# Moving the weight casts of a fused attention and expert kernel from its projection stage to the head of its attention stage, and doubling the final output buffer

## The reference, cut to what matters

```python
def _L0_attn_ref(x, Wq, bq, Wk, bk, Wv, bv, Wo, bo):      # 16 heads of 128, causal
    q = (x @ Wq.T + bq).reshape(B, S, nh, hd).transpose(0, 2, 1, 3)
    ...
    probs = jax.nn.softmax(scores, axis=-1)
    attn = jnp.einsum('bhqk,bhkd->bhqd', probs, v)
    y = attn.transpose(0, 2, 1, 3).reshape(B, S, H)
    return y @ Wo.T + bo

def _L0_ffn_ref(x, router_w, ...):                        # 8 experts, top 2
    ...
    combined = jnp.einsum('etf,te->tf', expert_out, full_w.reshape(-1, E)).reshape(B, S, D)
    out = jnp.einsum('bsd,df->bsf', combined, proj_w) + proj_b
    y = x + out
    rms = jnp.sqrt(jnp.mean(y * y, axis=-1, keepdims=True) + EPS)
    return norm_w * (y / rms)

xn = _layernorm(x, axis=-1)
x = x + _L0_attn_ref(xn, ...) + _L0_ffn_ref(xn, ...)
```

## Time and profile before

| | us |
|---|---|
| two timed executions | 5594.8 and 5755.85 |
| their median | 5675.32 |
| the profiled execution, its own time | 5243.77 |
| span of its slowest core, from first to last instruction | 5242.2 |
| spans of its 8 cores | 5219.3 to 5242.2 |

### The profile page before, as it was taken

How to read it: one execution, slowest core, us unless ns; L and a number is a source line. 1 busy time by engine, 2 the same in 40 slices (tenths; PEclk the granted TensorE clock), 3 DMA queues, 4 the chain that set the end, 5 groups by cost and what they waited for, 6 DMA issues and landing times.

```text
span 5242.2 us, 52589 instructions; the slowest of 8 cores (5219.3 to 5242.2 us)
## 1 busy us (share of the span) xinstructions
PE 4232.7 (81%) x18602; PEld 1734.9 (33%) x18602; DVE 1166.2 (22%) x1883; ACT 1007.8 (19%) x1781; POOL 336.3 (6%) x539
## 2 busy tenths in 40 slices
PE   0169999999634899999994448888988889897988
PEld 0134444444321344444442213333333332323333
DVE  2431111211121111211122122212131221314211
ACT  2511111111111111111112111230403214040400
POOL 1001111111011111111111100000000000000000
PEclk9999999999867899999997778998989989897899
DMA  8214444444866544444466830000000000001033
GB/s 126 81 29 65 69 69 69 69 69 68 134 125 131 90 69 68 69 69 69 69 97 135 149 104 17 17 9 25 5 21 13 13 21 5 25 9 60 26 121 121
DMA packets 223346, 339.65 MB, mean 65 GB/s; under 512 B 16578, under 2 KB 189042, under 8 KB 217714
## 3 DMA queue, kind: packets, MB, share of 16 engines
q0 software_dynamic: 156368, 201.47, 26.7%
q1 hardware_dynamic: 66722, 134.82, 8.0%
HBM read 487.34 MB, written 75.50 MB: 107 GB/s over the span
## 4 chain that ended last, share of the span: by engine, by line
PE 72%; DMA 12%; DVE 5%; DVEq 4%; ACT 3%; issue 2%; another core or an unknown queue 1%; ACTq 1%; SPq 0%; POOL 0%; POOLq 0%
PE pbk L243 72%; DMA wring<-pwb 7%; DVEq L129 4%; DMA xcst<-x 2%; DMA prt<-out 2%; ACT xnstg L375 1%; DVE wTst L693 1%; DVE WoT L759 1%; ACT rrow L813 1%; ACTq L129 1%; DVE pstg L616 1%; DMA xst<-x 1%; ACT rrow L816 0%; DVE finst L866 0%
## 5 line engine op out<-in xcount | busy, mean ns | idle before, releaser
L243 PE MATMUL pbk<-wring,xnT 128*128 128x512 bf16 x8192 | 1861.1, 380 | 65.8 <-DMA wring<-ew 64.0
L243 PEld LDWEIGHTS pbk<-wring,xnT 128*128 128x128 bf16 x8192 | 760.4, 98 | 1031.1 <-issue 187.3
L243 PE MATMUL pbk<-xnT,wTst 128*128 128x512 bf16 x3072 | 753.5, 411 | 0.0
L491 DVE SCALAR_TENSOR_TENSOR comb<-silu,fullw,comb 128x512 f32<-128x512 bf16 x448 | 336.7, 751 | 1400.6 <-ACT silu L479 1400.3
L791 ACT ACTIVATE PTs<-pbk 128x512 bf16<-128x512 f32 x640 | 382.3, 597 | 1335.5 <-PE pbk L243 1306.3
L479 ACT ACTIVATE silu<-pbk 128x512 bf16<-128x512 f32 x512 | 305.6, 597 | 1634.1 <-PE pbk L243 1600.5
L243 PEld LDWEIGHTS pbk<-xnT,wTst 128*128 128x128 bf16 x3072 | 320.2, 105 | 413.1 <-issue 109.7
L243 PE MATMUL pbk<-wring,cT 128*128 128x512 bf16 x1024 | 249.8, 407 | 185.0 <-DMA wring<-pwb 184.0
L248 POOL DMA_DIRECT2D wring<-ew x256 | 192.0, 750 | 2039.0 <-PE pbk L243 2039.0
L243 PE MATMUL pbk<-sIb,wring 128*128 128x128 bf16 x1024 | 118.0, 258 | 223.8 <-DVE wTst L693 125.4
L243 PE MATMUL pbk<-PTs,Vh 128*128 128x512 bf16 x640 | 257.6, 403 | 0.0
(11 more groups left out here) (100 smaller groups left out, 1869.3 us busy)
## 6 DMA issues: line engine op xcount, KB each, us to landing
wring<-ew POOLq DMA_DIRECT2D x256, 512.0 KB, 6.0
wring<-pwb SPq DMA_DIRECT2D x64, 512.0 KB, 8.3
wring<-wqk SPq DMA_DIRECT2D x64, 512.0 KB, 3.2
xcst<-x POOLq DMA_DIRECT2D x64, 256.0 KB, 4.4
out<-pstg SPq DMA_DIRECT2D x64, 256.0 KB, 3.0
prt<-out SPq DMA_DIRECT2D x16, 1024.0 KB, 6.8
out<-finst SPq DMA_DIRECT2D x16, 1024.0 KB, 4.7
xst<-x SPq DMA_DIRECT2D x32, 256.0 KB, 4.1
```

The costliest lines, as they stand in the source:

```text
L243: return eng.matmul(b, l, r, start=st, stop=sp)
L491: return e.scalar_tensor_tensor(co, silu_sb[ssl][:], wcol, co, ALU.mult, ALU.add)
```

## The change

**Where the casts are issued.** In the projection stage each of the 16 column blocks had four casts ahead of it, 64 in all. Now a list `EARLY` holds 12 of them (the rows of Wq, Wk and Wv for heads 0 to 3), and each of the first 12 blocks has one. The last four blocks have none. The other 52 stand in the attention stage, at the head of the loop over pairs of heads: those of two later heads for Wq, Wk and Wv, and two of Wo, in each pass.

**The output buffer.** `finst` has two buffers instead of one, used in turn, and their writes count on two semaphores.

```diff
@@ projection stage
+            EARLY = [w4 * n_dt + h4 for h4 in range(4) for w4 in range(3)]
             for c in range(n_fc):
-                qb = ((hf * n_q + q) * n_fc + c) * (4 * n_dt) // (2 * n_q * n_fc)
-                for qpc in range(qb, min(qb + (4 * n_dt) // (2 * n_q * n_fc),
-                                         4 * n_dt)):
+                slot = (hf * n_q + q) * n_fc + c
+                npsl = max(1, len(EARLY) // (2 * n_q * n_fc) + 1)
+                for qpc in EARLY[slot * npsl:(slot + 1) * npsl]:
                     dma(GPSIMD,
@@ attention stage
+    EARLYSET = set(w4 * n_dt + h4 for h4 in range(4) for w4 in range(3))
     for hp in range(NH // 2):
+        for w4 in range(4):
+            for h4 in (2 * hp + 4, 2 * hp + 5):
...
+                for hx in ([h4] if w4 < 3 else []):
+                    if hx < n_dt:
+                        qpc = w4 * n_dt + hx
+                        if qpc not in EARLYSET:
+                            dma(GPSIMD,
+                                dwqk[qpc * 128:(qpc + 1) * 128, :],
+                                [dWq, dWk, dWv, dWo][w4][
+                                    hx * 128:(hx + 1) * 128, :],
+                                "d_qkc", (), [("wqkp", qpc)])
+        for h4 in (2 * hp, 2 * hp + 1):
+            qpc = 3 * n_dt + h4
+            if qpc < 4 * n_dt:
+                dma(GPSIMD, dwqk[qpc * 128:(qpc + 1) * 128, :],
+                    dWo[h4 * 128:(h4 + 1) * 128, :],
+                    "d_qkc", (), [("wqkp", qpc)])
@@ output stage
     finst = [es_d.enter_context(nc.sbuf_tensor(f"finst{i}", [128, D], F32))
-             for i in range(1)]
+             for i in range(2)]
...
-                return e.tensor_add(finst[0][:, c * 512:(c + 1) * 512],
+                return e.tensor_add(finst[fsl][:, c * 512:(c + 1) * 512],
...
-        dma(SYNC, dout[i * 128:(i + 1) * 128, :], finst[0][:], "d_o20",
-            [("fin", 0, c2) for c2 in range(n_fc)], [("outdram2", i)])
+        dma(SYNC, dout[i * 128:(i + 1) * 128, :], finst[fsl][:],
+            f"d_o2{fsl}", [("fin", fsl, c2) for c2 in range(n_fc)],
+            [("outdram2", i)])
```

More of the change, by code:

```diff
@@ L673, in build_program @@
     vop(lambda e: e.memset(onescol[:], 1.0), (), [("onescol",)])
+    EARLYSET = set(w4 * n_dt + h4 for h4 in range(4) for w4 in range(3))
     for hp in range(NH // 2):
+        for w4 in range(4):
+            for h4 in (2 * hp + 4, 2 * hp + 5):
+                if w4 == 3:
+                    h4b = 2 * hp
+                    qpc = 3 * n_dt + h4b + (0 if hp % 1 else 0)
+                for hx in ([h4] if w4 < 3 else []):
[13 more added lines that the diff above has]
+                    "d_qkc", (), [("wqkp", qpc)])
         for hh in range(2):
@@ L841, in build_program @@
     finst = [es_d.enter_context(nc.sbuf_tensor(f"finst{i}", [128, D], F32))
-             for i in range(1)]
+             for i in range(2)]
     sch.handoff([("prt", 0), ("prt", 1)]
-                + [("fin", 0, c2) for c2 in range(n_fc)],
+                + [("fin", f2, c2) for f2 in range(2) for c2 in range(n_fc)],
                 CKEYS + LATEB)
@@ L864, in build_program, with f_fin @@
                [("onesb",), ("bor",)], [("pk", bank)])
-            def f_fin(e, bank=bank, c=c, psl=psl):
-                return e.tensor_add(finst[0][:, c * 512:(c + 1) * 512],
+            def f_fin(e, bank=bank, c=c, psl=psl, fsl=fsl):
+                return e.tensor_add(finst[fsl][:, c * 512:(c + 1) * 512],
                                     prt[psl][:, c * 512:(c + 1) * 512],
                                     pbk[bank][:, 0:512])
-            vop(f_fin, [("pk", bank), ("prt", psl)], [("fin", 0, c)])
-        dma(SYNC, dout[i * 128:(i + 1) * 128, :], finst[0][:], "d_o20",
-            [("fin", 0, c2) for c2 in range(n_fc)], [("outdram2", i)])
+            vop(f_fin, [("pk", bank), ("prt", psl)], [("fin", fsl, c)])
+        dma(SYNC, dout[i * 128:(i + 1) * 128, :], finst[fsl][:],
+            f"d_o2{fsl}", [("fin", fsl, c2) for c2 in range(n_fc)],
+            [("outdram2", i)])
     final_counts = sch.resolve()
```

## The result

The changed kernel is slower by 0.94%: the ratio to the kernel before is 1.0094, with a 95% interval of 1.0072 to 1.0115. That is a small loss, under the 2% that the prediction called the least that can be told from no change, but clear of 1. The lowest times are 5238.48 us before (of 42 executions) and 5293.09 us after (of 43). The plain medians, 5443.0 and 5314.27 us, say nothing of the change: in many executions of either kernel the cores of one die, sometimes of both, run at a lower TensorE clock and end up to 13% later, and the ratio leaves those out. The profiled execution took 5334.93 us, on a slowest core whose span is 5333.4.

A forecast was written before the change was run, and what follows sets the result against it. DMA engines were taken to bound the projection's column blocks, TensorE the rest of experts and attention. Terms -194 + 240 + 0 = +46 us, added to the timed median of 5675.3, gave 5721 us; range 5270 to 5850.

The forecast's parts named there:

- Rival D: Whole kernel: timed executions come out near the profiled level, or above today's timed ones; low case 5290 against 5675; chance 0.12.
- Part 1: Projection column blocks: casts taken out no longer delay the `pwb` loads, a gain of 194 us.
- Part 2: Start of attention: the first `wqk` load waits for all 52 casts behind the projection, a loss of 240 us.
- Part 3: Output stage: the second `finst` buffer changes nothing, since the `prt` load comes last; cost and gain 0.
- A: Start of attention: first `wqk` load waits for its own cast alone, leaving only the gain, 5050 or 5481 us; chance 0.04.
- B: DMA engines: a cast costs 5.8 us, more than in the first burst, sum +160 us, 5404 or 5835; chance 0.14.
- C: Output stage: the second buffer pays, removing 24.8 us of waits, sum +21 us, 5265 or 5696; chance 0.04.

The follow-up runs named there:

- the run without a burst: The changed kernel with its 52 late casts left out and the loads reading the rows of heads 0 to 3 instead: 5057.57 us in one execution.
- The half burst: The changed kernel with 26 of its 52 late casts left out, the rest still waited for at once: 5175.22 us in one execution.
- the wait by pair: The changed kernel with late Wq, Wk and Wv casts counted on a semaphore per pair of heads, Wo's on another: ratio 0.9905, lowest 5190.03 us.

## Why the prediction was right or wrong

**The time was wrong in its level.** The step that failed is the last one of the sum, "so I add the 46 us to their median". It took the median of two timed executions, 5675.3 us, for the kernel's own level, although the one execution with a trace stood at 5243.77. Of the 42 executions of the kernel before, the lowest is 5238.48, 19 are below 5330 and 19 above 5500, and both timed ones, 5594.8 and 5755.85, are among the latter. On the profiled execution's level the same sum gives 5290; measured are 5293.09 as the lowest, and 5334.93 for the execution with the profile. Rival D, which I held at 0.12, is what came.

**That 0.9% met 0.94% is in part luck.** In the mean of the 8 cores of the two profiles the terms are: 185 us gained before attention, where I had 194, and a wait for `wqk` that grew by 236 us, where I had 240. That makes 50 us more at the start of attention, against a forecast of 46. The mean span grew by 64 us, from 5230.8 to 5294.7. Of the 14 us that are left, 12 come from cores 6 and 7, which ran at a lower clock, and no term of mine stands for them.

**Part 1 (194 us) was right in its mechanism and some 9 us too high in the mean of the cores.** The windows of the slowest cores give 196.5, the run without a burst 176 to 184. The casts that stayed cost 7.9 to 14.4 us of waits for `pwb`, where I had 12. The 61.9 us that I gave the second and fourth quarter for a slow first block did not come: the fourth took 60.07, at a granted clock of 1.00. The 16.32 us of the earlier trace rows had followed a wait of 21.62 us for `pwb`, and that wait is gone.

**Part 2 (240 us) was right.** PE's wait is 300.3 to 308.6 us over the 8 cores against a forecast of 308, at 4.64 us a cast against 4.7. The half burst gives 4.4 and 4.7. The estimate of 4.39 us from the Trainium skill ("DMA: Bandwidth & Descriptors", Specifications) was 5% too low, and the 4.89 of the first burst, with loads of x beside it, 5% too high. One sentence of part 1 is wrong here: the tail of the last quarter did get casts beside it, and its writes took up to 49 us to land. In the changed kernel that is hidden under the wait for the count.

**Part 3 (0) was right,** and by the reason given: ratio 1.0007 for the buffer alone, and the adds still released by the `prt` load.

**The rivals.** A (the wait is not for all) is excluded by the wait itself. Had it been so, the kernel would not have stood at 5050, as I priced it, but at 5190, as the wait by pair showed. I had taken the DMA engines' idle time in attention as room for the burst, and overlooked SyncE's writes and loads at the stage's head, which come late beside it. B (5.8 us a cast) is refuted: 4.4 to 4.7. C is refuted by the second buffer alone.

## What to carry to other kernels

When transfers are moved, look at what the first consumer waits for: a semaphore counted to its total makes the first load pay for the last cast. Taking that wait away is half of the cure, since a backlog of casts on one queue also starves the small loads of the other; the transfers belong where the DMA engines have room and the other queue is silent, here the experts. A second buffer helps only if its release is what comes last, which one line of the waits tells.

## What the runs showed of the hardware that was not expected

A load of 0.5 MB on SyncE's queue, 3.2 us when alone, landed 74 to 119 us after its issue beside a backlog of casts on GpSimd's queue, and the loads behind the first followed at one in 21 to 24 us. Writes of 256 KB on the same queue, 2.6 us in the kernel before, took up to 50.8:

```profile
DMA to landing us min/median/max: 5.2/19.5/50.8
```

In the changed kernel's profiled execution cores 6 and 7 had a lower clock for a while after the hole. The windows from 3146 to 3340 us of core 7 and of core 0:

```profile
3146.00:3340.00 194.00, 170.47 (x650) 66.05 (x651) 45.69 (x64) 28.69 (x48) 0.00 (x0) 0.76 0.06 20
```

```profile
3146.00:3340.00 194.00, 161.06 (x688) 64.27 (x688) 45.68 (x64) 34.01 (x58) 0.00 (x0) 0.89 0.07 25
```

0.76 against 0.89, before both go on at 0.89 until 4930 us. In the rest, which is mostly the output stage, they part again. Core 7 is shown first:

```profile
4930.00:5333.00 403.00, 350.41 (x1356) 128.40 (x1355) 55.09 (x80) 53.66 (x90) 0.00 (x0) 0.93 0.27 84
```

```profile
4930.00:5333.00 403.00, 327.12 (x1324) 122.64 (x1322) 52.31 (x76) 45.50 (x76) 0.00 (x0) 0.97 0.24 84
```

From its first attention matmul to the end core 7 needs 2187.4 us and core 0 2141.5. Of these 46 us, some 20 are lost before the first add of the output stage and 26 behind it. Core 6 needs 2189.2 us, cores 0 to 5 need 2133.5 to 2143.0. What brought the lower clock on was not tried. It can't be the 300 us of idleness alone, since six cores had them too and did not show it.
